# Negated maxima of the attention folded in by products over 64 rows, right in front of each step's scores

## The reference

```python
q = (x @ Wq).reshape(b, s, N_HEADS, HEAD_DIM)      # 16 heads of 64
k = (x @ Wk).reshape(b, s, N_HEADS, HEAD_DIM)
v = (x @ Wv).reshape(b, s, N_HEADS, HEAD_DIM)
dot = jnp.einsum('bihd,bkhd->bhik', q, k)
w = jax.nn.softmax(dot / jnp.sqrt(jnp.float32(HEAD_DIM)), axis=-1)
a = jnp.einsum('bhij,bjhd->bihd', w, v)
a = a.reshape(b, s, N_HEADS * HEAD_DIM)
return a @ Wo + bo
```

## Time and profile before

| | |
|---|---|
| time before, median of 3 | 2023.5 us (2021.75 to 2027.29) |
| the profiled execution's own time | 2026.25 us |
| its span from first to last instruction | 2025.0 us |
| TensorE busy | 1767.8 us (87%) |
| VectorE busy | 1388.2 us (69%) |
| GpSimd busy | 1096.3 us (54%) |
| ScalarE busy | 789.5 us (39%) |
| L1665 / L1685 / L1691 / L1706 products | 1024 / 1024 / 6 groups of 2 a round / 2048 |

### The profile page before, as it was taken

The page is one execution under the profiler, slowest core; times in us unless marked ns, Lnnn a source line. Parts: engine busy times, 40 slices in busy tenths (PEclk is TensorE's granted clock), DMA queues, the critical chain, the costliest instruction groups (busy, mean ns, idle before and its releaser), DMA issues.

```text
span 2025.0 us, 35353 instructions
## 1 busy us (share of the span) xinstructions
PE 1767.8 (87%) x13602; PEld 969.7 (48%) x13602; DVE 1388.2 (69%) x2434; ACT 789.5 (39%) x1201; POOL 1096.3 (54%) x642
## 2 busy tenths in 40 slices
PE   4777764294899999999999999999999999995893
PEld 3656554282444444444444444444444444443383
DVE  3554556236777778777877778777877788776564
ACT  3343332162344444444444444444444444442131
POOL 2222220403476777677776777677766777783302
PEclk7656665596999999999999999999999999997897
DMA  7000000121000000000000000000000000003012
GB/s 238 3 3 3 3 2 1 37 61 29 1 1 1 1 1 1 1 1 1 1 1 1 1 1 1 1 1 1 1 1 1 1 1 1 1 1 97 31 54 62
DMA packets 41533, 32.76 MB, mean 16 GB/s; under 512 B 3604, under 2 KB 37392, under 8 KB 41368
## 3 DMA queue, kind: packets, MB, share of 16 engines
q1 hardware_dynamic: 31096, 22.12, 3.6%
q0 software_dynamic: 2048, 4.20, 0.7%
q10 hardware_dynamic: 8224, 4.19, 0.7%
HBM read 18.96 MB, written 11.53 MB: 15 GB/s over the span
## 4 chain that ended last, share of the span: by engine, by line
PE 80%; DVE 9%; issue 5%; POOL 3%; ACT 2%; DMA 1%; SPq 0%; DVEq 0%; POOLq 0%
PE psum L1706 22%; PE psum L1691 20%; PE psum L1665 8%; PE psum L1685 5%; PE psum L1332 2%; PE psum L1721 2%; PE psum L1715 2%; PE psum L1106 1%; PE psum L1638 1%; PE psum L1118 1%; DVE a_mx L1870 1%; PE psum L1292 1%; PE psum L340 1%; POOL a_acc L2002 1%; PE psum L403 1%
## 5 line engine op out<-in xcount | busy, mean ns | idle before, releaser
L2002 POOL TENSOR_TENSOR a_acc<-a_acc,a_Pb 128x832 f32<-128x832 f32 x448 | 893.6, 1995 | 307.2 <-ACT a_Pb L1808 274.5
L1870 DVE TENSOR_REDUCE a_mx<-psum 128x2 f32<-128x1024 f32 x512 | 625.1, 1223 | 237.0 <-PE psum L1665 234.0
L1808 ACT ACTIVATE a_Pb<-psum 128x1024 f32<-128x1024 f32 x512 | 496.7, 1022 | 702.5 <-PE psum L1691 702.5
L1706 PE MATMUL psum<-a_Pb,a_Vb 128*64 128x512 f32 x2048 | 494.3, 603 | 0.0
L1921 DVE TENSOR_TENSOR a_acc<-a_acc,a_Pb 128x192 f32<-128x192 f32 x448 | 230.0, 513 | 28.2 <-ACT a_Pb L1808 5.4
L1706 PEld LDWEIGHTS psum<-a_Pb,a_Vb 128*64 128x64 f32 x2048 | 127.1, 136 | 244.8 <-issue 173.4
L1665 PE MATMUL psum<-a_Kh,a_Qh 64*128 64x512 f32 x1024 | 231.0, 447 | 7.0 <-DVE a_mx L1870 6.9
L1691 PE MATMUL psum<-a_Qh,a_Kh 64*128 64x512 f32 x1024 | 230.7, 446 | 0.0
L1691 PE MATMUL psum<-a_Ql,a_Kh 64*128 64x512 f32 x1024 | 203.6, 392 | 0.0
L1691 PE MATMUL psum<-a_Qh,a_Kl 64*128 64x512 f32 x1024 | 203.0, 391 | 0.0
L1665 PEld LDWEIGHTS psum<-a_Kh,a_Qh 64*128 64x128 f32 x1024 | 96.9, 184 | 221.2 <-issue 209.9
(11 more groups left out here) (378 smaller groups left out, 2033.1 us busy)
## 6 DMA issues: line engine op xcount, KB each, us to landing
x_rows<-zero ACTq DMA_DIRECT2D x2, 2048.0 KB, 22.2
g_w<-in_L_ffn_w_eDF_dram SPq DMA_DIRECT2D x2, 1408.0 KB, 8.6
r_W<-in_L_ffn_W_dram SPq DMA_DIRECT2D x1, 2048.0 KB, 11.8
r_tile_x<-x_rows SPq DMA_DIRECT2D x16, 128.0 KB, 2.1
y_rows<-r_tile_y SPq DMA_DIRECT2D x16, 128.0 KB, 1.8
g_tile_x<-x_rows SPq DMA_DIRECT2D x16, 128.0 KB, 2.2
y_rows<-g_tile_y SPq DMA_DIRECT2D x16, 128.0 KB, 1.8
g_w<-in_L_ffn_w_eFD_dram SPq DMA_DIRECT2D x2, 512.0 KB, 10.7
```

Of the source, the lines that this page charges most:

```text
L1706: last = pe.matmul(ps[HEAD[h], B_O, :], b.Vb[:, p // 2 % 2, kc, at], b.Pb[:, step % BUFS, h * QT:(h + 1) * QT], start=(kc == 0), stop=(kc ...
L1808: act.activation(b.Pb[:, step % BUFS, :], ps[:, slot:slot + 2, :].rearrange("p a b -> p (a b)"), ACT.Exp, scale=SCALE).then_inc(S["probs"], 1)
L1870: v.tensor_reduce(b.mx[:, :, qc, quarter:quarter + 1], ps[:, bank:bank + 2, :], AX.X, ALU.max).then_inc(S[f"free{bank}"], 1)
L2002: g.tensor_tensor(b.acc[:, u, at], before, b.Pb[:, step % BUFS, at], ALU.add).then_inc(S["added_pool"], 1)
```

## The change

The products with the ones took 32 rows each: four of them, one in each quarter of the array, filled the four banks of a round in one go. They now take 64 rows, two of them fill the two banks of one step, and they stand directly in front of that step's three pairs. The wait for the probabilities that free the banks is split in the same way (`probs` at 2R - 1 for step 0, 2R for step 1). `nm` and `mask` hold the maxima once per head instead of twice, so the negation and the set-up of the pattern have half the instructions. VectorE's and GpSimd's shares of the sums are as they were.

```diff
-        if R:
-            pe.wait_ge(S["probs"], 2 * R)
-        for g in range(4):
-            rows = slice(32 * g, 32 * (g + 1))
-            pe.matmul(ps[:, 2 * (g % 2) + g // 2, :], b.ones[rows, :], b.Mr[rows, :], start=True, stop=False, tile_position=(32 * g, 0))
         for i in range(2):
             kc, slot = 2 * d + i, 2 * i
             at = slice(kc * P, (kc + 1) * P)
+            if R:
+                pe.wait_ge(S["probs"], 2 * R - 1 + i)
+            for h in range(2):
+                pe.matmul(ps[:, slot + h, :], b.ones[HEAD[h], :], b.Mr[HEAD[h], :], start=True, stop=False)
             for n, (K, Q) in enumerate(((b.Kh, b.Qh), (b.Kh, b.Ql), (b.Kl, b.Qh))):
...
-        for half in range(2):
-            nm = b.nm[:, :].rearrange("p (h x) -> p h x", h=2)[:, :, 32 * half:32 * half + 4]
-            last = v.tensor_reduce(nm, b.mx[:, :, :, :], AX.X, ALU.max, negate=True)
-        last.then_inc(S["negated"], 1)
+        nm = b.nm[:, :].rearrange("p (h x) -> p h x", h=2)[:, :, 0:4]
+        v.tensor_reduce(nm, b.mx[:, :, :, :], AX.X, ALU.max, negate=True).then_inc(S["negated"], 1)
...
-    for g in range(4):
-        rows = slice(32 * g, 32 * (g + 1))
-        dve.did(v.tensor_copy(b.mask[rows, :, :], bcast(k.ident[rows, 32 * g:32 * g + 4].unsqueeze(2), [32, 4, P])))
+    for h in range(2):
+        dve.did(v.tensor_copy(b.mask[h * D:h * D + 32, :, :], bcast(k.ident[h * D:h * D + 32, h * D:h * D + 4].unsqueeze(2), [32, 4, P])))
```

## The result

| | before | after |
|---|---|---|
| time, median (lowest to highest) | 2022.62 us (2021.21 to 2027.29), 4 runs | 2042.04 us (2039.88 to 2045.92), 4 runs |
| ratio, 95% interval | | 1.0094 [1.0071, 1.0117] |
| span of the profiled execution | 2025.0 us | 2040.4 us |
| TensorE / VectorE / GpSimd busy | 1767.8 / 1388.2 / 1096.3 us | 1726.8 / 1434.5 / 1094.1 us |

The account below looks back on a forecast made before the run. TensorE was taken to bound the attention, with GpSimd and VectorE nearly full in d = 5 to 7. From 2026.25 us, 42 saved and 82 lost to held adds gave 2066; range 1979 to 2090.

Parts of the forecast that it names:

- The saving of TensorE: TensorE's products in rounds with a late maximum: 0.17 us shorter in each of 247 rounds, 42 us.
- The block between the adds: VectorE's add issued while GpSimd's runs is held to that add's end and 0.21 us more.
- The price of a miss at d = 6: VectorE's second add held for a whole GpSimd add delays the next late maximum to 6.04 us: 1.63 lost; d = 7: 1.37.
- the count of misses: Held second adds at d = 6 in 31 units, at d = 7 in 3 of 4: 2.66 us a unit, 82 us.
- rival 2: One held add per unit, at d = 6 or d = 7, against the 42 us saved: 2023 to 2033 us; chance 0.25.
- The whole saving (1): TensorE's saving comes through whole, the block between VectorE and GpSimd being misread: 1982 us; chance 0.20, whole or nearly so.
- The fall of the clock (3): Long waits lower TensorE's clock; another 1.5 us in every unit would give 2121 us; chance 0.08.
- Rival 4: TensorE's 0.44 distances are not from changing rows, so a 0.23 us pair per round is added: 2080 us; chance 0.05.
- the rule on the shared port: By the skill's rule VectorE's add waits for GpSimd's; the sum itself went by the profile's rows.

Follow-up runs that it names:

- experiment 1: Both kernels with GpSimd adding only 64 of its 832 columns, except in each unit's first add (wrong sums): changed 1973.55 us, before 2018.43 us.
- fixing the order (3): Changed kernel, with GpSimd's add of each even step waiting for VectorE's adds of the round before: 1997.53 us, 0.9865.
- 8: VectorE adds both steps in one instruction, TensorE sums the two partial sums by one more product a unit: changed 1984.12 us, before 2032.40 us.
- 9: Changed kernel, VectorE adding both steps in one instruction and folding the two partial sums by one more add per unit: 1975.56 us, 0.9768.
- 7: Changed kernel plus an idle pair of 384-column products on TensorE in front of each early maximum: 2019.42 us, 0.9983.
- experiment 6: Kernel before, without the third pair (Kl x Qh) of each round's second step: 2063.62 us, 1.0204.
- experiments 5: Changed kernel with both pairs of ones products at the head of the round, after one wait: 2055.05 us, 1.0156.

## Why the prediction was right or wrong

**The saving of TensorE** (0.17 to 0.18 a round, 42 us) was right: 44.9 us in experiment 1, by the distances that were forecast, 0.34 and 0.23. The last unit, with its rounds without a late maximum and with the same split wait, took 29.3 us to its last round, and 29.2 before, so nothing was saved or lost there to speak of.

**The block between the adds** was right, and it decides: fixing the order (3), taking the second add away (8, 9) or giving the time back (7) each takes the 58.5 us of waits of L1665 down to 1.7 or less, and experiment 6 makes the same loss with the old ones products.

**The price of a miss at d = 6** was right: 6.00 to 6.03 against 6.04. Against the 4.37 that the round takes without a miss it is 1.63 to 1.66. At d = 7 it was right too: 6.20 against 4.80 is 1.40, where 1.37 stood.

**The step that failed** is the count of misses: one at d = 6 in all 31 units and "I count it in 3 of 4 units" for d = 7, with 2.66 us a unit, 82 us. What the misses cost, by place, is the difference of the round lengths between the changed kernel and its version of experiment 1, over units 0 to 30:

| | forecast | measured |
|---|---|---|
| d = 6 | 31 misses, 50.5 us | 25 misses, 40.5 us |
| d = 7 | 23 misses, 31.8 us | 6 misses, 9.3 us |
| d = 2 to 5 | none | 15 misses, 17.4 us |
| d = 0 and 1 | none | no miss, 0.6 us |
| all rounds | 82 us | 46 misses, 67.8 us |

Two things were wrong in it. First, d = 7. In units 0 to 23 it missed once, and most of these units paid the 1.63 of d = 6 alone, which is rival 2. I had the second add at 2.64 us behind the late maximum and GpSimd at 2.59, so the add 0.05 too late. At 1263.11 the add comes at 2.565 and GpSimd at 2.570. Nearly all of the 0.075 by which the add is earlier is the reduction behind the reciprocal, 1.15 long where I took 1.23 from the earlier trace rows; there was no row of this situation in the trace before. A tie of hundredths was priced as a near-certain loss.

Second, I costed all 31 units alike, with d = 5 to 7 as the only nearly full rounds. From unit 24 on d = 3 is short as well, so the first miss moves to d = 4, where the queries' job covers part of it (6.00 instead of 5.28), and one or two more follow. That the values' job ends with unit 24 stands in the kernel's description. It is also why rival 2's own 2023 to 2033 was too low.

The two errors partly cancel, so 2066 lies nearer to 2042 than the count deserves. By the measured terms units 0 to 30 are 67.8 us longer by misses and 44.6 shorter by TensorE's saving (the difference of the two kernels of experiment 1). The change also took away 5.0 us that the kernel before had itself lost to the same block, most of it in unit 23; the forecast left this in. That makes +18.2. Unit 31, to its last round, adds 0.1, the attention began 2.1 us earlier in that execution (first ones products at 518.9 instead of 521.1), and what follows the last ones products took 0.8 less: 15.4, as between the spans.

**The rivals.** The whole saving (1) holds once the adds cannot meet, as experiments 1 and 9 show with 1974 to 1976 us. The fall of the clock (3) did not occur in the changed kernel, whose waits were 1.60 us or shorter. Why is not shown: in experiments 5 and 6 falls came behind some waits of 1.8 and 2.0 us and not behind others, and in experiment 6 behind two of 1.61 and 1.41 us as well, so the length of the wait alone does not decide. Rival 4 is out.

**What the rule on the shared port gave.** The Trainium skill (Advanced Engine Details and Errata, Mode Summary) says that VectorE's second SBUF port is shared with GpSimd, and that GpSimd's instructions and VectorE's two-port ones block each other. Whether this add is a two-port one no run shows. That the two engines' adds block each other the traces do show, and they give the time: an add of 192 columns that is issued while GpSimd's runs ends 0.21 to 0.22 us behind the end of GpSimd's, so one issued 13 ns behind GpSimd's start takes 2.17 us.

## What to carry to other kernels

Where two engines block each other, ask of each pair of instructions which starts first, by how much, and what moves both; busy shares and even the length of a gap do not tell. A faster bounding engine shortens the gaps of all that follow its rhythm, so a saving can cost more than it brings, and a tie of under 0.1 us should be forecast as open, one way and the other. The cure is to remove the race. One instruction instead of two short ones let the saving come through whole here (1975.56 us); a wait that fixes the order brought 44.5 of the 68.5 us back. And where a job exists in only a part of the units, cost those units apart.

## What was unexpected of the hardware

- A few ns decided 1.4 us: at d = 7 the second add started between 26 ns ahead of GpSimd's and 4 ns behind it in units 2 to 23 (unit 19 aside) and took 0.36 us; in five of the units from 24 on it started 7 to 21 ns behind and took 2.14 to 2.15 us.
- Work added to the bounding engine made the kernel 22.6 us faster (7), and work removed made it 40 us slower (6).
- 51 waits of at most 1.6 us left TensorE's clock at 2.4 GHz. Behind some waits of 1.8 and 2.0 us, and behind two of 1.41 and 1.61 in a kernel that had longer ones too, it fell to 1.2 GHz for a part of the next round.
- A reduction of 1024 columns behind a reciprocal took 1.15 us instead of 1.23 after the held add; the cause stays open.
